# A graph network kernel on one core: the table that steers a build turn is read in two parts instead of one

## What is computed

```python
edge_index = jnp.stack([src, dst])
h = jnp.maximum(_layernorm(x, axis=-1), 0.0)
x = x + _L0_gnn_ref(h, edge_index, ...)          # SAGE, two convolutions: mean over neighbours
h = jnp.maximum(_layernorm(x, axis=-1), 0.0)
x = x + _L1_gnn_ref(h, edge_weight, W, b, src, dst)   # GCN: weighted sum over neighbours
h = jnp.maximum(_layernorm(x, axis=-1), 0.0)
x = x + _L2_gnn_ref(h, edge_attr_64, src, dst, ...)   # interaction: sum of messages with edge features, MLP
h = jnp.maximum(_layernorm(x, axis=-1), 0.0)
x = x + _L3_gnn_ref(h, W_self, W_neigh, src, dst)     # top-32 features of each row, mean over neighbours
```

## Time and profile before

| | us |
|---|---|
| median of 3 runs | 1649.49 |
| lowest and highest run | 1647.69, 1650.51 |
| the profiled execution, its own time | 1648.47 |
| its span (first to last instruction) | 1645.9 |
| PE busy in it | 1571.8 (95%) |
| PEld busy | 1231.4 (75%) |
| DVE busy | 967.3 (59%) |
| ACT busy | 620.7 (38%) |
| POOL busy | 327.5 (20%) |

### The profile page before, as it was taken

How to read it: one execution, slowest core, us unless ns; L and a number is a source line. 1 busy time by engine, 2 the same in 40 slices (tenths; PEclk the granted TensorE clock), 3 DMA queues, 4 the chain that set the end, 5 groups by cost and what they waited for, 6 DMA issues and landing times.

```text
span 1645.9 us, 42637 instructions
## 1 busy us (share of the span) xinstructions
PE 1571.8 (95%) x11401; PEld 1231.4 (75%) x11402; DVE 967.3 (59%) x2866; ACT 620.7 (38%) x1693; POOL 327.5 (20%) x927
## 2 busy tenths in 40 slices
PE   7899998999999999999999999999999999998996
PEld 7555555555567777778888888888888888886885
DVE  6888897888861222243335666666646777777111
ACT  6777787777741111111112222222224444441000
POOL 1565565665530000000000000000002222220000
PEclk9999999999999999999999999999999999999998
DMA  4366585766698776533345666666632222131344
GB/s 138 91 183 161 154 208 145 186 177 161 170 243 229 224 206 188 173 115 124 119 156 148 165 165 165 165 166 168 172 110 71 76 83 83 62 137 65 120 142 154
DMA packets 353545, 245.62 MB, mean 149 GB/s; under 512 B 195242, under 2 KB 337382, under 8 KB 353510
## 3 DMA queue, kind: packets, MB, share of 16 engines
q1 hardware_dynamic: 353510, 245.19, 52.3%
HBM read 138.17 MB, written 99.31 MB: 144 GB/s over the span
## 4 chain that ended last, share of the span: by engine, by line
issue 60%; PE 32%; DVE 3%; POOL 3%; DVEq 1%; SPq 0%; POOLq 0%; DMA 0%; ACT 0%
PE ps L1429 22%; PE ps L1522 8%; POOL work L675 3%; PE ps L1471 1%; DVE e_buf L1021 1%; PE ps L1464 0%; DVE work L967 0%; DVE e_buf L1017 0%; SPq L424 0%; PE ps L1708 0%; DVE e_buf L1037 0%; DVEq L396 0%; DVEq L1017 0%; DVEq L1021 0%; PE ps L1402 0%
## 5 line engine op out<-in xcount | busy, mean ns | idle before, releaser
L1522 PE MATMUL ps<-arena 128*128 128x256 f16 (+1 forms) x5000 | 602.4, 272 | 6.6 <-DVEq L320 1.6
L1522 PEld LDWEIGHTS ps<-arena 128*128 128x128 f16 x5000 | 484.7, 97 | 101.3 <-issue 32.6
L1429 PE MATMUL ps<-e_buf 128*128 128x400 bf16 (+1 forms) x2476 | 381.2, 307 | 30.1 <-DVE e_buf L1021 20.3
L1429 PEld LDWEIGHTS ps<-e_buf 128*128 128x128 bf16 x2476 | 213.0, 97 | 190.7 <-DVE e_buf L1021 64.7
L1516 PE MATMUL ps<-arena 128*128 128x256 f32 x1250 | 278.7, 380 | 2.4 <-DMA arena<-wgt_blocks 2.4
L1516 PEld LDWEIGHTS ps<-arena 128*128 128x128 f32 x1250 | 235.8, 190 | 33.7 <-issue 1.7
L675 POOL TENSOR_TENSOR work<-work 128x256 f32<-128x256 f32 x75 | 59.8, 797 | 957.9 <-ACT work L860 957.9
L1021 DVE TENSOR_SCALAR e_buf<-iota,off_g,front 128x400 bf16<-128x400 f16 (+1 forms) x619 | 231.0, 416 | 32.6 <-PE ps L1429 20.5
L660 POOL TENSOR_SCALAR e_buf<-e_buf,w_col 128x128 bf16<-128x128 bf16 x600 | 216.6, 375 | 165.8 <-DVE e_buf L1017 165.4
L701 ACT ACTIVATE e_buf<-e_buf,front 128x128 bf16<-128x128 bf16 x219 | 88.0, 402 | 108.4 <-DVE e_buf L1017 108.2
L1017 DVE TENSOR_SCALAR e_buf<-iota,front 128x128 bf16<-128x128 f16 x419 | 102.0, 251 | 35.5 <-PE ps L1429 23.4
(11 more groups left out here) (215 smaller groups left out, 1585.7 us busy)
## 6 DMA issues: line engine op xcount, KB each, us to landing
arena<-turned_blocks SPq DMA_DIRECT2D x75, 800.0 KB, 4.3
wgt_blocks<-arena SPq DMA_DIRECT2D x25, 1600.0 KB, 10.3
arena<-wgt_blocks SPq DMA_DIRECT2D x25, 1600.0 KB, 8.7
cnt_blocks<-work SPq DMA_DIRECT2D x25, 800.0 KB, 5.5
turned_blocks<-arena SPq DMA_DIRECT2D x25, 800.0 KB, 3.8
e_raw<-edge_features_padded SPq DMA_DIRECT2D x25, 576.0 KB, 3.9
edge_features_padded<-in_edge_attr SPq DMA_DIRECT2D x24, 512.0 KB, 9.9
out<-arena SPq DMA_DIRECT2D x24, 128.0 KB
```

What stands on the lines that cost most here:

```text
L1429: return pe.matmul(bank[:, 0:wide], rows_, cols, start=start, stop=True, skip_group_check=True)
L1522: m = pe.matmul(into[:, 0:wide], counts[:, b * P:(b + 1) * P], ZH[zin(i)][:, b * ZW + part * D:b * ZW + part * D + wide], start=(b == 0 an ...
```

## The change

Every engine now reads half of its values at pair 0 and the other half at pair 4. The preparation writes the table in another order, so that one read of DVE still finds its rest and fixed values side by side. The number of values read in a turn stays the same; the number of TENSOR_LOAD instructions doubles on each of the four engines (25 to 50), and each is half as large (DVE 8 values, the others 4).

```diff
+HALF = PER // 2
...
-        def pairs_of(e, kind, c, which):
+        def pairs_of(e, kind, c, i, which):
...
-            lo, many = (0, PER) if which == "rest" else (PER, PER) if which == "fixed" else (0, 2 * PER)
-            at = c * (2 * PER) + lo
+            lo, many = (0, HALF) if which == "rest" else (HALF, HALF) if which == "fixed" else (0, PER)
+            at = c * (2 * PER) + (i * 2 + lo)
...
# POOL; ACT and PE in the same way
-                packed = pairs_of(pool, mybir.EngineType.Pool, c, "fixed")
                 for i in range(PER):
-                    weigh_pair(c, i, packed[i])
+                    if i % HALF == 0:
+                        packed = pairs_of(pool, mybir.EngineType.Pool, c, i, "fixed")
+                    weigh_pair(c, i, packed[i % HALF])
...
# the preparation
-            both = tab[0:1, 0:4 * P].rearrange("o (c a i) -> o c a i", a=2, i=PER)
+            both = tab[0:1, 0:4 * P].rearrange("o (c a i) -> o c a i", a=2, i=HALF)
...
# DVE
-                packed = pairs_of(dve, mybir.EngineType.DVE, c, "both")
                 for i in range(PER):
-                    hot_pair(c, i, packed[i], packed[PER + i])
+                    if i % HALF == 0:
+                        packed = pairs_of(dve, mybir.EngineType.DVE, c, i, "both")
+                    hot_pair(c, i, packed[i % HALF], packed[HALF + i % HALF])
                     if i == 3 and not isinstance(c, int):
                         own_take(c - 1)
```

More of the change, by code:

```diff
@@ L723, in chunk @@
             def chunk(c, half, par):
-                packed = pairs_of(act, mybir.EngineType.Activation, c, "rest")
                 for i in range(PER):
-                    weigh_pair(c, i, packed[i])
+                    if i % HALF == 0:
+                        packed = pairs_of(act, mybir.EngineType.Activation, c, i, "rest")
+                    weigh_pair(c, i, packed[i % HALF])
                     if i == 1:
@@ L1001, in _ @@
             dve.wait_ge(s_prep_pe, PE_TABLES + 2)
-            both = tab[0:1, 0:4 * P].rearrange("o (c a i) -> o c a i", a=2, i=PER)
+            both = tab[0:1, 0:4 * P].rearrange("o (c a i) -> o c a i", a=2, i=HALF)
             for k in range(2):
                 chain(dve.tensor_copy(both[:, :, k, :], ps[0:1, 2, k * 2 * P:(k + 1) * 2 * P].rearrange(
-                    "o (c i) -> o c i", i=PER)))
+                    "o (c i) -> o c i", i=HALF)))
             chain(dve.tensor_copy(tab[0:1, 4 * P:6 * P], ps[0:1, 3, 0:2 * P]))
@@ L1476, in _ @@
             with long_loop(pe, NT) as c:
-                packed = pairs_of(pe, mybir.EngineType.PE, c, "rest")
                 for i in range(PER):
-                    build_pair(c, i, packed[i])
+                    if i % HALF == 0:
+                        packed = pairs_of(pe, mybir.EngineType.PE, c, i, "rest")
+                    build_pair(c, i, packed[i % HALF])
                     if i == 4:
```

## The result

| | us |
|---|---|
| before, median of 4 runs | 1648.59 |
| after, median of 4 runs (1704.28 to 1710.71) | 1707.38 |
| ratio after to before | 1.0357 [1.0343, 1.0371] |
| the profiled execution after, its time and its span | 1710.71, 1708.9 |

The change makes the kernel 58.8 us slower. The forecast was 6.6 us slower, with a range that ended at 1659.0. The sign was right and the size was missed by a factor of nine.

A forecast was written before the change was run, and what follows sets the result against it. DVE's sequencer stream was taken to bound the build turn. Pair 4 (+15.7 us), behind the read (+1.5) and head (-10.6) sum to +6.6 on 1648.47: 1655.1 us, own range 1652 to 1658, wider range 1648.0 to 1659.0.

The forecast's parts named there:

- term 2, *Pair 4: At pair 4, DVE's new read makes the narrow Q start 0.63 us later, 15.7 us lost over 25 turns.
- what a half read costs: DVE's read of 8 values priced at 0.68 us, on the line through its reads of 1 and 16; low bound 0.55.
- the free split: Rival: DVE reads 8 values in 0.55 to 0.59 us; +0.1 to +2.1 us, about 1650 us; chance 0.20.
- What bounds the kernel now: In an ordinary build turn DVE's sequencer stream sets the length; PE follows with a few tenths of a microsecond to spare.
- Term 1, Head: At the turn's head, DVE's read shrinks from 1.105 to 0.68 us, all 0.425 gained: 10.6 us over 25 turns.
- Term 3, Behind the read: Behind DVE's read at pair 4, the sequencer no longer runs ahead: 0.06 us a turn lost, 1.5 us in all.
- The edits at nothing: Reads of PE, ACT and POOL at pair 4, PE's at the head, and the preparation's copies: covered, cost nothing.
- PE as the bound: Rival: PE's own read at pair 4 decides, 0.3 us lost there, 0.16 gained at the head; +3.5 us, 1652; chance 0.10.
- PE as the bound all along: Rival: DVE's lead swallows its read at pair 4, PE gains 0.34 us a turn; -8.5 us, 1640 us; chance 0.10.

## Why the prediction was wrong

**The step that failed** is term 2, *Pair 4*. It priced a read by what the same engine's reads took elsewhere, and none of those lay in a store out of SBUF: the reads of 16 values lay in the quiet, 46 of the 50 single ones in loads into SBUF, which do not slow a read. It put 0.63 us on the path at pair 4, and 1.92 came. The read takes 1.97 us where the forecast had 0.68, and the narrow Q came 2.25 us behind the start of `own_take` (264.96 to 267.21) instead of 0.33. In the section on what a half read costs, nothing asks what runs beside the new place of the read. The trace of before did show the traffic there, but it had no read inside it, and no rival named contention. The range took both ends of the unknown cost from rows outside any store, and so was far too narrow. Its ends are also looser than its sums: the free split at its low bound gives 1648.6, not 1648.0, a read of 0.64 to 0.72 us gives 1653.1 to 1657.1, not 1652 to 1658, and for 1659.0 no sum is given. None of this would have reached 1707.

**Where the 58.8 us went.** The slow reads: 24 turns x (1.97 - 0.60) = 32.9 us. The split itself, with quick reads at pair 4: 9.2 us of build (the kernel with the weight store later). The clock: 13.2 us by the medians, up to 17.0 by the traces (the kernel with products of zeros). Together 55.3 with the smaller number. The slow reads of PE, ACT and POOL can fill the other 3.5 us (2.7 to 5.8, the kernel that splits DVE alone). The parts are from different kernels and sum only to within a few us. The first is confirmed by turns: 17.45 us with PE kept busy against 16.12 with quick reads, 1.33 us, where the reads differ by 1.37. And 24 turns of the full 58.8 would be 2.45 us each; an ordinary turn shows 1.63, a turn with the clock at half 3.3 or more. The forecast had no term for the clock.

**What bounds the kernel now.** Right, and the experiments bear it out: splitting DVE alone gives the change's loss nearly whole (53.0 of 58.8 us), and moving engine work under the read gives nothing. The forecast saw the sequencer's stream as the bound of an ordinary turn. Yet it credited `own_take` with 0.4 us of cover for the read at pair 4. That is right for when the narrow Q starts, but no gain for the turn, as the kernel with `own_take` moved shows.

**What a half read costs.** Wrong: 600 ns in the quiet, not 680. The single reads were taken as the fixed part plus one value, but one value costs nearly as much as four (0.31 and 0.35 us), so the line through 1 and 16 values lies too high at 8; one through 4 and 16 gives 0.60. The rival *the split is free* had nearly the right price (0.55 to 0.59). Its time, 1650, would still have missed: with quick reads at pair 4 the turn grew by 0.30 us, not by 0.08 at the most. That the forecast's 6.6 us are near the 9.2 of that kernel's build is in part luck: with 0.60 its own terms give 25 x (0.55 + 0.06 - 0.505) = 2.6 us, and the price set too high stood in for a loss behind the read that was set too low.

**Term 1, Head.** About right: idle time 1.26 to 0.82 us, 0.44 gained where 0.425 was said, though 0.505 of the read fell away.

**Term 3, Behind the read.** Too small. With quick reads the narrow Q of pair 4 comes 0.87 us behind `own_take`'s start (258.17 to 259.04 us in the kernel with the weight store later), 0.33 before, so 0.54 for the read; less 0.44 at the head leaves 0.10 a turn, and measured are 0.30. The other 0.2 us are lost behind the read, where 0.06 was said. In the changed kernel the timeline of DVE there reads:

```profile
267.53 0.26 DVE L1020 TENSOR_SCALAR e_buf<-iota,front 128x128 bf16<-128x128 f16 x1
268.06 0.34 DVE L1020 TENSOR_SCALAR e_buf<-iota,front 128x128 bf16<-128x128 f16 x1 [0.28 <-issue]
```

The engine waits 0.28 us for its sequencer between the first two S of the pair, which ran as one group before.

**The edits at nothing.** PE's and the others' reads stayed mostly behind DVE's lateness as said (2.7 to 5.8 us of 58.8). But PE's new idle time was not free: filling it with products kept the granted clock at its full level and gave back 13.2 us or more. The forecast counted PE as a follower, whose waits pass on at one for one; where the clock fell behind them, the turn lost 1.6 us or more beyond the slow read.

**PE as the bound, and PE as the bound all along.** Both fell. PE's products wait for DVE's Q for 72.1 us in the changed kernel.

The Trainium skill's floor of about 600 ns for such a load (DMA: Bandwidth & Descriptors, section on latency and other measured facts) does not hold here: 4 values take 0.31 us on ACT and 0.35 on DVE in the quiet. DVE's 8 values, at 0.60 us, only happen to lie at it.

## What to carry to other kernels

Before a read of SBUF by a sequencer is moved or split, ask what the DMA engines do at its new place, not only what the engine does: the same instruction cost 0.60 us in the quiet and 1.97 us in a store. Price a moved instruction by rows that lie in the same kind of traffic, and where the trace has none, treat its price as unknown and widen the range. Read control values in the stretch of a turn in which no store out of SBUF runs, and in few large reads: the second read at pair 1 takes nearly all of the loss away, but the whole read of before is still no slower. And when PE is made to wait at a new place, look whether its granted clock falls behind it.

## What the runs showed of the hardware

- On DVE a load of registers from SBUF takes about three times as long while a DMA store reads SBUF: 4 values 0.35 against 1.01 and 1.07 us, 8 values 0.60 against 1.97, 16 values 1.105 against 3.66; 2 values, 0.53 against 2.19 to 2.34, take four times as long, and so do ACT's 8, 0.548 against 2.162. A copy from HBM to HBM (4 values 0.349, 16 values 1.107, at 261 to 289 GB/s) does not slow it, nor does a load into SBUF (1 value 0.31 to 0.32 at 341 GB/s, 16 values 1.109). By which path the two meet was not shown.
- In the quiet such a load takes 0.31, 0.53, 0.35, 0.60 and 1.105 us on DVE for 1, 2, 4, 8 and 16 values: 2 cost more than 4, and other sizes were not read.
- A load of registers on DVE's sequencer lengthens the turn by its whole time: added reads of 2.13 and 3.82 us made it 2.32 and 4.02 us longer. An operation of 0.40 us put ahead of it on the engine covers nothing: idle time at the head 1.24 us against 1.26, turn 15.82 us in both.
- After PE had been idle for 1.44 and 1.33 us with four products between, its granted clock stood at 0.5 for 3.4 us. This came in ten of 24 turns, and waits of much the same length passed without it in thirteen. Products of zeros in the idle time kept the clock at 1.00, which gave back 13.2 us by the medians.
